# Low weight parts of expert 0 made on VectorE alone, in other batches of the attention stage

## The reference

```
x: (8, 256, 512), ctx: (8, 256, 512), 16 experts, 4 of them for each token
n  = layernorm(x)
score = sigmoid(einsum('bdn,bdm->bnm', n, ctx) / 16)
x1 = x + tanh(g_xattn) * einsum('bvn,bnm->bvm', ctx, score)
t  = rmsnorm(layernorm(x1)) * norm_w
logits = t @ gate_w.T + gate_b ; top 4, softmax over the 4 -> G
h  = t @ w1[e].T + b1[e] ; a = min(h[::2], 7), b = clip(h[1::2], -7, 7)
y  = (a * sigmoid(1.702 a) * (b + 1)) @ w2[e].T + b2[e]
out = x1 + tanh(g_ffn) * (layernorm(x1) + sum over e of G[e] * y)
```

## Time and profile before

| what | value |
|---|---|
| median of 3 executions | 843.23 us (842.14 to 843.66) |
| the profiled execution's own time | 844.3 us |
| its span, first to last instruction | 842.5 us |
| mean granted TensorE clock | 0.959 of full speed |
| TensorE busy, matmuls | 766.3 us, 91% |
| VectorE busy | 520.2 us, 62% |
| ScalarE busy | 459.7 us, 55% |
| GpSimd busy | 317.8 us, 38% |
| stage one: last put ends | 164.7 us |
| first matmul of the expert loop | 179.8 us |

### The profile page before, as it was taken

How to read it: one execution, slowest core, us unless ns; L and a number is a source line. 1 busy time by engine, 2 the same in 40 slices (tenths; PEclk the granted TensorE clock), 3 DMA queues, 4 the chain that set the end, 5 groups by cost and what they waited for, 6 DMA issues and landing times.

```text
span 842.5 us, 16653 instructions
## 1 busy us (share of the span) xinstructions
PE 766.3 (91%) x4028; PEld 654.3 (78%) x4029; DVE 520.2 (62%) x1020; ACT 459.7 (55%) x785; POOL 317.8 (38%) x290
## 2 busy tenths in 40 slices
PE   5999997059999999999999999999999999999984
PEld 2666575048888899988888888898998988898873
DVE  3898885425676575566576665756556575746540
ACT  3565654025566564556557655646556565656540
POOL 0266775631324315242324333334333333325212
PEclk9998998568999999999999999999999999999997
DMA  7656663042577576347649645556535555544223
GB/s 283 196 193 201 210 177 114 10 131 78 128 210 172 111 215 162 62 129 207 137 149 230 174 104 130 147 137 154 145 67 146 107 150 134 155 124 75 37 25 38
DMA packets 107767, 117.00 MB, mean 139 GB/s; under 512 B 11808, under 2 KB 77344, under 8 KB 107744
## 3 DMA queue, kind: packets, MB, share of 16 engines
q1 hardware_dynamic: 88896, 77.32, 29.7%
q0 software_dynamic: 18848, 39.40, 23.8%
HBM read 88.06 MB, written 28.94 MB: 139 GB/s over the span
## 4 chain that ended last, share of the span: by engine, by line
PE 76%; DVE 7%; POOL 6%; issue 5%; ACT 3%; DMA 1%; another core or an unknown queue 0%; DVEq 0%; POOLq 0%; ACTq 0%
PE ps L543 41%; PE ps L492 25%; POOL tab L1138 5%; PE ps L471 4%; PE ps L407 3%; PE ps L395 2%; PE ps L390 1%; DVE uu L1062 1%; DVE hv L1064 1%; DVE W1l L1073 1%; ACT bw L711 1%; DVE bv L1060 1%; ACT hTh L731 1%; DMA xg<-rows,srcI 0%; PE ps L424 0%
## 5 line engine op out<-in xcount | busy, mean ns | idle before, releaser
L543 PE MATMUL ps<-xTh,W1h 128*128 x768 | 257.9, 336 | 13.8 <-issue 11.5
L543 PE MATMUL ps<-xTl,W1h 128*128 x768 | 252.2, 328 | 0.0
L543 PE MATMUL ps<-xTh,W1l 128*128 x768 | 252.0, 328 | 0.0
L1220 POOL DMA_INDIRECT out<-ys,dgI x75 | 118.9, 1585 | 309.9 <-ACT ys L690 287.0
L543 PEld LDWEIGHTS ps<-xTh,W1h 128*128 128x128 f32 x768 | 146.0, 190 | 24.7 <-issue 19.6
L543 PEld LDWEIGHTS ps<-xTl,W1h 128*128 128x128 f32 x768 | 146.1, 190 | 5.3
L543 PEld LDWEIGHTS ps<-xTh,W1l 128*128 128x128 f32 x768 | 145.8, 190 | 5.5
L492 PE MATMUL ps<-W2h,hTh 128*128 x300 | 119.8, 399 | 7.7 <-DVE hTl L1068 7.7
L690 ACT ACTIVATE ys<-ps,dgI 128x512 f32<-128x512 f32 x75 | 51.6, 689 | 121.9 <-DVE ps L1033 115.8
L492 PE MATMUL ps<-W2l,hTh 128*128 x300 | 117.6, 392 | 0.0
L492 PE MATMUL ps<-W2h,hTl 128*128 x300 | 117.5, 392 | 0.0
(11 more groups left out here) (140 smaller groups left out, 1066.5 us busy)
## 6 DMA issues: line engine op xcount, KB each, us to landing
W1f<-in_wts SPq DMA_DIRECT2D x64, 512.0 KB
W2f<-in_wts SPq DMA_DIRECT2D x32, 512.0 KB
X<-in_x SPq DMA_DIRECT2D x8, 512.0 KB
Kt<-in_ctx SPq DMA_DIRECT2D x8, 512.0 KB
Vt<-in_ctxT SPq DMA_DIRECT2D x8, 512.0 KB
rows<-tt SPq DMA_DIRECT2D x8, 512.0 KB
out<-base SPq DMA_DIRECT2D x8, 512.0 KB
b2s<-in_bias SPq DMA_DIRECT2D x16, 256.0 KB
```

What stands on the lines that cost most here:

```text
L543: m = e.matmul(P_[i % 2][:, 0:32 * w], (W1h, W1l)[wl][:, i, 2 * k + h, :], (xTh, xTl)[xl][:, bass.ds(par, 1), k, 0:32 * w], start=(t == 0) ...
L1220: e.indirect_dma_start(out, bass.IndirectOffsetOnAxis(dgI[:, j, 0:1].bitcast(I32), axis=0), ys[j][:], None, compute_op=ALU.add).then_inc(d ...
```

## The change

GpSimd makes no low part any more. VectorE makes all four of W1, piece b - 1 in batch b for b = 1 to 4, and both of W2 in batch 7, at the same place of its order as before (behind `places`, ahead of Kl; batch 7 has no Kl). The semaphore e_lop is gone: e_lo1 counts the four parts one by one, SP's wait in batch b is for b - 2 of them, and TensorE's wait ahead of stage two is dropped.

```
@@ sp
-                    e.wait_ge(*((e_lop, 1), (e_lo1, N1), (e_lop, 2), (e_lop, 3))[b - 3])
+                    e.wait_ge(e_lo1, b - 2)
@@ pe
-            e.wait_ge(e_lop, 3)
@@ dve, low
-                    e.tensor_tensor(W1l[:, c, :, :], W1f[:, c, :, :], W1h[:, c, :, :].bitcast(F32), ALU.subtract).then_inc(e_lo1, N1)
+                    e.tensor_tensor(W1l[:, c, :, :], W1f[:, c, :, :], W1h[:, c, :, :].bitcast(F32), ALU.subtract).then_inc(e_lo1, 1)
@@ dve, loop over b
-                if b in (2, 5, 6):
-                    low((1, 4, 5)[(2, 5, 6).index(b)])
+                if 1 <= b <= N1:
+                    low(b - 1)
+                if b == B - 1:
+                    low(N1)
+                    low(N1 + 1)
@@ pool
-            def low(c):
-                e.wait_ge(e_hi1, c + 1)
-                e.tensor_tensor(W1l[:, c, :, :], W1f[:, c, :, :], W1h[:, c, :, :].bitcast(F32), ALU.subtract).then_inc(e_lop, 1)
-
@@ pool, loop over b
-                if b in (1, 3, 4):
-                    low((0, 2, 3)[(1, 3, 4).index(b)])
```

More of the change, by code:

```diff
@@ L239, in build @@
         v_wa, v_wc, v_rf = sem("v_wa"), sem("v_wc"), sem("v_rf")
-        e_hi1, e_lo1, e_lop, e_hi2, e_lo2, e_b1, e_bc, e_go = (sem(n) for n in ("e_hi1", "e_lo1", "e_lop", "e_hi2", "e_lo2", "e_b1", "e_bc", "e_go"))
+        e_hi1, e_lo1, e_hi2, e_lo2, e_b1, e_bc, e_go = (sem(n) for n in ("e_hi1", "e_lo1", "e_hi2", "e_lo2", "e_b1", "e_bc", "e_go"))
         e_tx, e_xh, e_xl = sem("e_tx"), sem("e_xh"), sem("e_xl")
```

## The result

Over 20 executions of each, the changed kernel takes 837.88 us (835.54 to 842.13) and the kernel before 843.03 us (841.04 to 845.94): ratio 0.9941, 95% interval 0.9929 to 0.9953, some 5.0 us faster. The forecast was 838.1. The changed kernel's profiled execution took 837.56 us (span 835.8).

The account below looks back on a forecast made before the run. The first stage was read as a race of TensorE and GpSimd, whose puts wait for a VectorE stalled by GpSimd's subtractions. Terms 2.3 + 2.8 = 5.1 us off the median 843.23 gave 838.1 us, range 836.0 to 841.2.

Parts of the forecast that it names:

- The terms 2.3 and 2.8: Batches 3 and 4: without VectorE's stalls, put(1) starts 2.3 us earlier and put(2) another 2.8 us.
- the rule of two SBUF inputs: Trainium skill: a VectorE instruction with two SBUF inputs contends with a GpSimd SBUF read; the second blocks completely.
- Batch 1, batch 2, and the waits: First batches and semaphore waits: counted as nothing; without TensorE's cover batch 1 would gain up to 1.0 us.
- Batches 5 and 6: Each loses a VectorE subtraction of 1.13 us; earns nothing, since GpSimd sets the pace there.
- Batch 7: Two added VectorE subtractions, 2.3 us, fit into 3.4 us of idle time: cost nothing, uncovered up to 2.3 us.
- I take it that the clock then stays at 1.00: Batch 4: with TensorE's idle 1.14 us shrunk to about 0.3, its granted clock no longer falls to 0.50.
- Rival 1: Batch 4: TensorE's clock falls all the same, some 2.6 of 5.1 us remain, 840.7 us; chance 0.12.
- rival 2: Batches 1 to 4 and 7: VectorE's total work becomes the bound, gain 0.6 us, 842.6 us; chance 0.10.
- rival 3: Batches 3 and 4: VectorE's subtractions hold GpSimd's puts by 0.8 us each, 839.7 us; chance 0.08.
- the inference named in the prediction: Puts: generating descriptors needs only the write interface, so a two-input VectorE subtraction would cost a put nothing.
- rival 4: Start of the expert loop: four more matmul groups run cold, 2.7 us slower, 845.9 us; chance 0.04.
- The unnamed wait of 1.50 us: Before Lg at 140.05, releaser unknown, on the path to put(6); if it goes, 836.6 us, a range end.

Follow-up runs that it names:

- c2_only: Kernel before, with only GpSimd's subtraction of batch 3 moved to VectorE; ratio to before 0.9971.
- c3_only: Kernel before, with only GpSimd's subtraction of batch 4 moved to VectorE; ratio to before 0.9976.
- pool_double: Kernel before, with GpSimd's subtraction of batches 3 and 4 made twice in a row; ratio to before 1.0049.
- c2_c3: Kernel before, with GpSimd's subtractions of batches 3 and 4 moved to VectorE, second-layer parts left in batches 5 and 6; ratio to before 0.9942.
- w1_only: Changed kernel with the second-layer parts back in batches 5 and 6, so only first-layer parts move; ratio to before 0.9940.
- late_tts: Changed kernel with one more ScalarE copy ahead of tTs in batch 3, so TensorE idles before the logits; ratio to before 0.9938.
- before_again: Kernel before, profiled again without an edit; put(6) starts 96.23 us behind put(0), no ratio given.
- w2_tail: Changed kernel with the two second-layer parts made behind the batches, ahead of the last choose, instead of in batch 7; ratio to before 0.9971.
- w2_only: Kernel before, with only the second-layer parts moved from batches 5 and 6 to batch 7; ratio to before 1.0004.
- pool_fill: Changed kernel with a GpSimd memset of 128x2048 where its subtraction stood in batches 3 and 4; ratio to before 0.9942.

## Why the prediction was right

**The bound and the stall.** Right. Put(1) was forecast at 63.4 and came at 63.44, put(2) at 78.8 and 78.69; TensorE's batch 5 at 86.0 and 86.02, batch 7 near 117 and 116.65. The terms 2.3 and 2.8 measured 2.3 and 2.9 on the put distances (17.22 to 14.93, and 35.40 to 30.18 less that), c2_only and c3_only split them, a second subtraction adds 1.8 and 2.0 more (pool_double), and the timed sum is 5.0 against 5.1. That the sum is so close is in part luck, since two things behind put(2) that were put at nothing offset each other: see batches 5 and 6, and batch 7. The reading that 6.2 us are lost in batches 3 and 4 "and nowhere else" is wrong: TensorE starts batches 3 to 7 at 55.22, 72.48, 90.17, 106.94 and 122.11, which is 2.1, 2.5 and 1.6 us over 15.17 in batches 3, 4 and 5. And the rule of two SBUF inputs that the prediction says explains the stalls fits ex; c has one tensor input, and was held all the same.

**Batch 1, batch 2, and the waits.** Nothing, as said: c2_c3 has 0.9942 with batch 1 left on GpSimd.

**Batches 5 and 6.** The sum was right, the detail not. I took VectorE's lighter load to earn nothing, since GpSimd sets the pace. Puts(3) and (4) became 0.7 and 0.8 us shorter (10.75 and 10.71 against 11.46 and 11.54 in w1_only), because no wide operation stands right behind dst: the first put took 1.03 instead of 1.76. It earned nothing because TensorE ended the path there; TensorE, and not GpSimd, bounds the changed kernel from here on. Its start of batch 7 stands 73.60 us behind put(0) before the change and 68.14 after: 5.5 us gained, against 5.2 at put(2).

**Batch 7.** Right: 0.61 and 1.82 us of idle time are left. Counted from TensorE's start of the batch, both sums are 0.5 us later than before (9.88 and 14.19 us against 9.37 and 13.68), because TensorE's value product is; in late_tts, with the same pair, neither is late (9.40 and 13.68). That takes back what batches 5 and 6 gave.

**The clock.** The step "I take it that the clock then stays at 1.00" had the right outcome and a wrong reason. The idle time of 1.14 us did not bring the clock down in four other profiles, and where it fell, in the first profile, it cost put(2) nothing. Rival 1, priced at 2.5 us, was laid to the wrong place: the one fall on the path in the kernel before (1.2 to 1.5 us at put(4)) came behind the longer idle time of batch 4 in before_again, and the changed kernel has no idle time above 0.2 us ahead of its logits.

**VectorE as the bound** (rival 2). It still waits 0.36 us for rs1 in batch 4. **Held puts** (rival 3). Puts(1) and (2) took 11.4 and 11.6 us in the changed kernel against 11.5 and 11.9, so zero was right in batches 3 and 4. Its price of 0.8 us is not general: w2_tail shows 2.3, which also speaks against the inference named in the prediction that such a subtraction costs a put nothing. **Slower** (rival 4). Not seen; the mean granted clock is 0.965 against 0.959.

**Put(6)** was forecast near 139.6 and came at 138.19. The unnamed wait of 1.50 us explains most of it: the distance fell by 6.5 us (96.18 to 89.68), of which 5.5 came by TensorE's start of batch 7, 1.5 is the wait, and 0.5 was lost in batch 7. The wait was in one of two profiles of the kernel before, in w2_tail (1.77) and pool_double (0.93), and not in either of the changed kernel. What it is stays open.

## What to carry to other kernels

When a tiny instruction takes microseconds, look at what the neighbouring engine runs in the same microseconds: the price of moving 2.4 us of work to an idle-looking GpSimd was paid by VectorE, on the path. A replay of one stage, with each hand-over between engines and the durations of the rows, gave each of the two stalls within 0.2 us, where busy shares (GpSimd 38%, VectorE 62%) would have argued for the opposite. And ask of a striking event in one profile, a slow clock or an unnamed wait, whether a second profile of the same kernel has it.

## What was not expected of the hardware

The granted clock fell behind an idle time of 1.14 us in one profile and stayed at 1.00 behind 1.15, 1.15, 1.15 and 1.18 us in four others; behind 2.41 us it fell (0.53 over 87.5 to 92 us) in before_again, and behind 2.42 us it fell in w2_only as well, but only 2.9 us after the idle time had ended, and for 3 us. Both idle times of pool_double, 2.91 and 3.16 us, were followed by a fall too. So every idle time over 2.4 us in the middle of the batches had one, and of the five of about 1.15 us one; when it comes, and whether it is on the path, differed between profiles with the same idle time. What decides that is open.

The same pair of VectorE subtractions held the first of eight puts by some 0.8 us in batch 7 of the changed kernel (1.76 us at 123.94), where it started ahead of the put, and by 2.3 us in w2_tail, where the put started 0.09 us ahead of it. The order of the starts is one difference; no run tested it alone.

A tiny operation with one tensor input (c, 3.04 us) was held as those with two were, in batch 4, and again in w2_only and before_again (3.00 and 2.99 us). It is recorded as starting 0.6 us ahead of GpSimd's subtraction (78.35 against 78.97), and ex in batch 3 0.1 us ahead (61.17 against 61.27), so a held operation can look like the earlier one. Another operation with one tensor input, jj, took 0.41 us under a memset, which reads nothing, in pool_fill; it took as long beside a put at 146.44 in the changed kernel, so what holds it is not shown. Which operation is caught depends on when it is issued: in c2_only, c passed and ex was held.
